# A decoder layer on one core: the first attention's feature maps shared between VectorE and GpSimd

## What is computed

```python
def _feature_map(t, K):                       # 16 heads of 64
    f = jnp.einsum('hdf,bhld->bhlf', K, t)
    feats = jnp.concatenate([jax.nn.softmax(f, axis=-1), jax.nn.softmax(-f, axis=-1)], axis=-1)
    return jnp.maximum(feats, EPS)
q, k, v = _heads(x @ Wq), _heads(x @ Wk), _heads(x @ Wv)
qf, kf = _feature_map(q, Kq), _feature_map(k, Kk)
kv = jnp.cumsum(kf[:, :, :, None, :] * v[..., None], axis=2)
o = jnp.einsum('bhlf,bhldf->bhld', qf, kv)
z = jnp.einsum('bhlf,bhlf->bhl', qf, jnp.cumsum(kf, axis=2)) + EPS
y = heads_joined(o / z[..., None]) @ Wo       # x = x + y
```

## Time and profile before

| | |
|---|---|
| median of 3 runs | 1230.46 us (1229.52 to 1231.06) |
| the profiled execution | 1229.25 us, span 1227.0 us |
| the first attention | about 540 us of it |
| TensorE clock granted, mean | 0.982 of full speed |
| busy share of the span | TensorE 91%, VectorE 78%, ScalarE 50%, GpSimd 31% |

### The profile page before, as it was taken

How to read it: one execution, slowest core, us unless ns; L and a number is a source line. 1 busy time by engine, 2 the same in 40 slices (tenths; PEclk the granted TensorE clock), 3 DMA queues, 4 the chain that set the end, 5 groups by cost and what they waited for, 6 DMA issues and landing times. The chain is left out here.

```text
span 1227.0 us, 30062 instructions
## 1 busy us (share of the span) xinstructions
PE 1117.3 (91%) x11860; PEld 719.6 (59%) x11861; DVE 962.1 (78%) x1769; ACT 611.1 (50%) x1166; POOL 377.3 (31%) x355
## 2 busy tenths in 40 slices
PE   6698898899899999879999999999999957999996
PEld 5577777777788878643443344334444334666765
DVE  6889978987888788888788677877889556777757
ACT  4233343334333433227777677776788822444443
POOL 4432245222522222113201320222110414656651
PEclk9899999999999999999999999999999988999998
DMA  7100001000400000524720570065050144221225
GB/s 240 41 8 1 2 28 53 2 1 1 80 2 2 1 1 2 81 59 81 152 34 8 114 146 2 9 127 108 2 211 3 53 80 145 65 64 60 63 62 205
DMA packets 60045, 73.65 MB, mean 60 GB/s; under 512 B 14404, under 2 KB 51140, under 8 KB 59188
## 3 DMA queue, kind: packets, MB, share of 16 engines
q1 hardware_dynamic: 56132, 61.56, 21.0%
q0 software_dynamic: 3792, 10.36, 2.7%
HBM read 52.86 MB, written 18.78 MB: 58 GB/s over the span
## 5 line engine op out<-in xcount | busy, mean ns | idle before, releaser
L1791 DVE TENSOR_REDUCE neg_max<-pS 128x1 f32<-128x1024 f32 x238 | 284.9, 1220 | 56.2 <-PE pS L1574 56.0
L1706 ACT ACTIVATE pt<-pR 128x512 f32<-128x512 f32 x512 | 286.5, 600 | 80.1 <-PE pR L1597 75.3
L1597 PE MATMUL pR<-qs,ks 100*32 100x512 bf16 x2048 | 191.2, 383 | 3.1 <-ACT pt L1706 1.6
L1574 PE MATMUL pS<-ks,qs 100*32 100x512 bf16 x1904 | 145.9, 381 | 5.1 <-issue 1.9
L1611 PE MATMUL b_pO<-pt,b_v 128*32 128x512 f32 x1024 | 135.9, 605 | 2.9 <-ACT pt L1706 2.3
L1597 PEld LDWEIGHTS pR<-qs,ks 100*32 100x32 bf16 x2048 | 56.2, 96 | 95.3 <-issue 25.6
L324 POOL TENSOR_TENSOR kf<-kf,fsum 128x2048 f32<-128x2048 f32 (+1 forms) x17 | 58.2, 3422 | 163.8 <-DVE fsum L933 163.8
L324 POOL TENSOR_TENSOR qs<-qs,fsum 128x2048 f32<-128x2048 f32 (+1 forms) x17 | 58.5, 3446 | 142.7 <-DVE fsum L933 142.7
L1453 POOL COPY qs<-max_rows 3x512 bf16<-3x512 bf16 x60 | 36.6, 610 | 209.3 <-ACT max_rows L1699 206.3
L745 ACT COPY qfT<-pT 128x512 f32<-128x512 f32 x64 | 37.3, 582 | 122.7 <-PE pT L466 122.7
L1574 PEld LDWEIGHTS pS<-ks,qs 100*32 100x32 bf16 x1904 | 51.4, 97 | 74.3 <-issue 35.7
(11 more groups left out here) (376 smaller groups left out, 2270.8 us busy)
## 6 DMA issues: line engine op xcount, KB each, us to landing
qs<-q_scr SPq DMA_DIRECT2D x24, 256.0 KB
ks<-k_scr SPq DMA_DIRECT2D x7, 768.0 KB
k_scr<-f SPq DMA_DIRECT2D x18, 256.0 KB, 2.8
ks<-in_L_ffn_w_dram SPq DMA_DIRECT2D x2, 2048.0 KB, 11.1
ks<-in_L_ffn_w_dram SPq DMA_DIRECT2D x4, 1024.0 KB, 8.5
ks<-y_rows SPq DMA_DIRECT2D x16, 256.0 KB, 5.1
ks<-k_scr SPq DMA_DIRECT2D x6, 512.0 KB
cx<-in_ctx_dram SPq DMA_DIRECT2D x3, 768.0 KB, 12.3
```

What stands on the lines that cost most here:

```text
L1574: ins = pe.matmul(pS1[q:q + XV, slot, 512 * half:512 * half + 512], qs[0:KR, bass.ds(par, 1), h, P * t + q:P * t + q + XV].rearrange("r a ...
L1597: ins = pe.matmul(ring[bank][q:q + XV, :], ks[0:KR, bass.ds(par, 1), h, P * j + q:P * j + q + XV].rearrange("r a n -> r (a n)"), qs[0:KR, ...
L1706: nc.scalar.activation(pt[:, j % 2, i, :], ring[bank], ACT.Exp).then_inc(exp_done, 1)
L1791: nc.vector.tensor_reduce(neg_max[:, hg % 2, u // G, u % G:u % G + 1], pS1[:, u % 2, :], AX_X, ALU.max, negate=True).then_inc(max_done, 1)
```

## The change

From tile 2 of the keys and tile 1 of the queries on, VectorE writes only the positive side, and min - max of each head; GpSimd makes the negative side as (min - max) - (f - max) from it, in SBUF (`other_side`), and ScalarE's exponentials wait for that. A new semaphore `drained` frees the half of `pP` for TensorE as soon as VectorE has read it. GpSimd also takes the clamps of all tiles but 0; the queries' product and clamp are done in halves of eight heads. VectorE's clamps leave its loop. The keys' sums stood ahead of the residual and the mask in the kernel before as well (L1121).

```diff
+        low_less_high = sb("low_less_high", [P, 2, H])
+        drained = [sem("k_drained"), sem("q_drained")]
+        POOL_FROM = (2, 1)
+        def bank_drained(eng, m, t, half_of):
+            if t < POOL_FROM[m]:
+                eng.wait_ge(shifted[m], 2 * t + half_of + 1)
+            else:
+                eng.wait_ge(drained[m], 2 * (t - POOL_FROM[m]) + half_of + 1)
...
+                def scaled_after(m, t, part):
+                    if m == 1:
+                        return 2 * t + part + 1
+                    return t + part + 1 if t == 0 else t + 2
+                def clamp(m, t, par, hs=slice(0, H), part=1):
+                    pool.wait_ge(scaled[m], scaled_after(m, t, part))
+                    nc.gpsimd.tensor_scalar(feat[m][:, par, hs], feat[m][:, par, hs], FEAT_EPS, None,
+                                            ALU.max).then_inc(f_ready[m], 1)
+                def other_side(m, t, half_of, par):
+                    pool.wait_ge(drained[m], 2 * (t - POOL_FROM[m]) + half_of + 1)
+                    hs = slice(8 * half_of, 8 * half_of + 8)
+                    nc.gpsimd.tensor_tensor(feat[m][:, par, hs, HD:F2],
+                                            low_less_high[:, m, hs].unsqueeze(2).broadcast_to([P, H // 2, HD]),
+                                            feat[m][:, par, hs, 0:HD], ALU.subtract).then_inc(shifted[m], 1)
...
-                        if not (last and c == TB - 1):
-                            scale(1, TB * b + c + 1, (c + 1) % 2)
+                        if has1:
+                            other_side(1, t + 1, 0, 1 - par)
+                            clamp(0, t + 1, 1 - par)
+                            other_side(1, t + 1, 1, 1 - par)
+                            for half_of, hs in enumerate(HALVES):
+                                scale(1, t + 1, 1 - par, hs, half_of)
+                                clamp(1, t + 1, 1 - par, hs, half_of)
                         if (b, c) == (0, TB - 1):
                             split_k(0)
                             split_k(1)
-                        if not (last and c >= TB - 2):
-                            scale(0, TB * b + c + 2, c % 2)
+                        if has2:
+                            other_side(0, t + 2, 0, par)
+                            other_side(0, t + 2, 1, par)
+                            scale(0, t + 2, par)
...
                 def project_q(t, half, par):
-                    wait(pe, shifted[0], 2 * t + half + 1)
+                    bank_drained(pe, 0, t, half)
...
-                    nc.vector.tensor_tensor(feat[m][:, par, hs, 0:HD], f,
-                                            hi[:, m, hs].unsqueeze(2).broadcast_to([P, H // 2, HD]), ALU.subtract)
+                    if t >= POOL_FROM[m]:
+                        nc.vector.tensor_tensor(low_less_high[:, m, hs], lo[:, m, hs], hi[:, m, hs], ALU.subtract)
+                    ins = nc.vector.tensor_tensor(feat[m][:, par, hs, 0:HD], f,
+                                                  hi[:, m, hs].unsqueeze(2).broadcast_to([P, H // 2, HD]),
+                                                  ALU.subtract)
+                    if t >= POOL_FROM[m]:
+                        ins.then_inc(drained[m], 1)
+                        return
...
-                            if g == 1 and has1:
-                                clamp(0, t + 1, 1 - par)
...
-                            if g == G - 1 and has1:
-                                clamp(1, t + 1, 1 - par)
```

More of the change, by code:

```diff
@@ L320, in scale @@
                 def scale(m, t, par, hs=slice(0, H), part=1):
-                    wait(pool, summed[m], t + part + 1)
+                    wait(pool, summed[m], t + part + 1 if t == 0 else t + 2)
                     e = feat[m][:, par, hs].rearrange("p h (s f) -> p (h s) f", s=2)
@@ L377, in batch @@
                                                     ).then_inc(x1_norm, 1)
-                        if not (last and c == TB - 1):
-                            scale(1, TB * b + c + 1, (c + 1) % 2)
+                        t, par = TB * b + c, c % 2
+                        has1, has2 = not (last and c == TB - 1), not (last and c >= TB - 2)
+                        if has1:
[5 more added lines that the diff above has]
+                                clamp(1, t + 1, 1 - par, hs, half_of)
                         if (b, c) == (0, TB - 1):
@@ L448, in project_q @@
                 def project_q(t, half, par):
-                    wait(pe, shifted[0], 2 * t + half + 1)
+                    bank_drained(pe, 0, t, half)
                     project(1, half, par, proj[1])
                 def project_v(t, half, par):
-                    wait(pe, shifted[1], 2 * t + half + 1)
+                    bank_drained(pe, 1, t, half)
                     project(2, half, par, v_proj)
@@ L458, in transposes @@
                     for m in (1, 0):
-                        if t == 0 and g % 2 == 0:
-                            wait(pe, f_ready[m], g // 2 + 1)
+                        if m == 1 and g % 2 == 0:
+                            pe.wait_ge(f_ready[m], 2 * t + g // 2 + 1)
+                        elif t == 0 and g % 2 == 0:
+                            pe.wait_ge(f_ready[m], g // 2 + 1)
                         elif g == 0:
-                            wait(pe, f_ready[m], t + 2)
+                            pe.wait_ge(f_ready[m], t + 2)
+                        if g == 0:
                             wait(pe, oT_ready, 2 * t)
@@ L927, in denominators @@
                     if t:
-                        wait(dve, scaled[m], t + 1)
+                        wait(dve, scaled[m], 2 * t if m == 1 else t + 1)
                     d = fsum[:, m, 2 * hs.start:2 * hs.stop]
```

## The result

The changed kernel takes 1318.65 us (median of 4 runs, 1315.38 to 1319.62), the kernel before 1229.99 beside it (4 runs, 1229.06 to 1231.06). The ratio is 1.0716, with a 95% interval of 1.0695 to 1.0737: 7.2% slower, or 88.7 us by the medians. The forecast was 1246.8 with a range up to 1258. The sign was right and the size wrong by a factor of five. The profiled execution has a span of 1316.1 us, against 1227.0 before.

What follows compares the result with a forecast made beforehand. The prediction took TensorE, nearly full at 91% busy, as the bound, with VectorE binding tiles 1 and 2. Its tile terms summed to +16.3 us on 1229.25, giving 1245.6; with 1.2 for the median, 1246.8, range 1235 to 1258.

Steps and rivals of the forecast that it cites:

- predicted +6.4: Tiles 4 and 8: negative query side issued behind two splits on GpSimd, clamp of 2.3 us included; +6.4 us each.
- price of a side: GpSimd's negative side of 512 columns, from the line through two product prices: 1.04 us.
- balance of the ordinary tiles: Later mask +0.35 us against state wait gone -0.55: -0.2 in tiles 6 and 10, 0 in 7 and 11.
- The rival in which the relief wins: Queue effects cost little and state waits of 12.4 us go: -10 us, 1220; chance 0.10.
- GpSimd's prices: GpSimd's clamp, priced between memset and two-input rows: 2.3 us whole, 1.45 a half.
- Behind the sums: After the query sums, half products and clamps take 6.8 us on GpSimd; first key side needed some 7 later: just hidden.
- two-input price adds about 9.5: Range term: clamps at the two-input price add about 9.5 us, 1.3 in tiles 0, 4, 5, 8, 9, 13.
- relief of tiles 1 and 2: Tiles bound by VectorE, making mask rows too; shorter state and mask waits give -2.7 and -2.0 us.
- the last pair: Last two tiles: waits for the first row maximum (1.17) and the state (0.4) shrink, about 1.5 us gained.
- Contention: VectorE and GpSimd block each other; by it alone tiles 5, 9 and 13 would each cost some 0.3 us more.

Runs made afterwards that it cites:

- The first experiment: Changed kernel with both clamps back on VectorE and the query product whole again, GpSimd keeping the negative sides: 1247.10 us, ratio 1.0108.
- the splits' order: Kernel with only the negative sides on GpSimd, the splits of tiles 4 and 8 moved behind the query sides: 1240.21 us, ratio 1.0073.
- two-input price: Changed kernel with GpSimd's clamp replaced by a two-tensor addition of the clamp's constant over the same columns: 1281.51 us, ratio 1.0389.
- normalisation later: Changed kernel with VectorE's normalisation issued one head group later, behind the division of group 1: 1304.99 us, ratio 1.0567.
- the clamps only: Changed kernel with the negative sides back on VectorE, GpSimd keeping the clamps: 1234.74 us, ratio 1.0014.
- sides, query clamp: Changed kernel with the keys' clamp back on VectorE, GpSimd keeping the negative sides and the queries' clamp: 1263.24 us, ratio 1.0269.
- clamp behind sides: Changed kernel with GpSimd's keys' clamp placed behind both negative query sides instead of between them: 1273.98 us, ratio 1.0342.
- key clamp, norm. later: Kernel with negative sides and only the keys' clamp on GpSimd, VectorE's normalisation moved behind the division of group 1: 1300.13 us, ratio 1.0559.
- sides, key clamp: Changed kernel with the queries' clamp back on VectorE, GpSimd keeping the negative sides and the keys' clamp: 1306.52 us, ratio 1.0621.
- those of the key sums: VectorE's key sums moved behind residual, mask and statistics: on the kernel before 1230.17 us; on the sides-only kernel with splits behind the sides 1251.18 us.

## Why the prediction was wrong in size

**What held.** The order of the mechanism: a negative side behind other work in GpSimd's queue delays the exponential, then the sums, the mask and TensorE. The first experiment gives 1247 for the sides, and the splits' order alone gives back 5 us in tile 4 and 4.6 in tile 8. That their +6.4 and +6.0 equal the predicted +6.4 is luck, since no clamp stands in them. The price of a side (1.04) held, and so did the balance of the ordinary tiles as long as the clamps stay on VectorE: tiles 6 and 7 changed by -0.2 and +0.1 (unrounded) with the sides alone, where -0.2 and 0 were predicted. The rival in which the relief wins is excluded by the time. The relief is not nothing: with the sides alone TensorE's waits for the state fell from 12.4 us (7.5 and 4.9 in the earlier trace rows) to 6.0. In the changed kernel they are 15.7 and 6.8.

The stage by groups of tiles, each against the kernel before, in us (the two last columns are taken from the residual additions; tile 0 is what is lost ahead of the first of them):

```
tiles             predicted   two-input price   changed
0                   +2.4          +6.6           +9.6
1, 2                -4.7          +1.5           +7.1
3                   +4.1          +7.0          +10.5
4, 8               +12.8         +16.6          +22.8
5, 9, 13            +4.4         +13.0          +20.1
6, 7, 10, 11        -0.4          +6.1          +13.5
12                  -0.7          +3.2           +6.0
14, 15              -1.5          -0.1           +3.1
sum                +16.3         +53.9          +92.6
```

**"GpSimd's prices" failed.** The clamp is 5.36 us, not 2.3, and a half 2.77, not 1.45. The upper end was wrong too: the product with two inputs was taken to bound an instruction with one. By the addition in the clamp's place, the part above the two-input price is worth about 40 us; by the table of stretches below, 23 of the 36 us that it adds to the stage are TensorE's busy time, that is the clock's.

**"Behind the sums" failed with it.** Products and clamps in halves last 9.5 us against 6.8, and the key sides come behind them: the query clamp adds 1.6% over the sides.

**The range's "two-input price adds about 9.5" failed on its own.** With the step at 3.61 us the loss is 48, where the sum gave 26. By the table, tiles 4 and 8 are then nearly right (8.3 each, where 7.7 were predicted at that price), and what is missing lies elsewhere. First, in the ordinary tiles the clamp between the two query sides was left out, as if the second side did not want GpSimd until the clamp had ended: tiles 6, 10 and 12 lose 2.8, 2.8 and 3.2 us (7 and 11, which have no state update, 0.4 and 0.1). At the prediction's own 2.3 us this would have cost next to nothing (an estimate: with the normalisation later, a clamp of 2.3 from 288.43 would end at 290.73, and the side's values, but for the hold, would be there at about 290.7); so the omission and the wrong price hang together. Second, the relief of tiles 1 and 2, put at -4.7, and of the last pair, at -1.5, did not come. The two state waits of the earlier trace rows stand at 1.71 and 1.56 us with the sides alone, as they stood before, and no kernel gained more than 0.7 us in tiles 1 and 2 together, or 1.3 in the last pair. Why they stayed was not looked for.

**The clamp's place was worth as much as its price.** Moving the clamp behind the second query side, at its full price, takes back 3.8% (7.2 to 3.4), 46 us, some 4 in eleven of the tiles (tile 6 goes from 34.8 to 31.1). The lower price in the old place took back 40. The two overlap and don't add up: what is lost is a wait as long as the clamp, at the one place where the query side needs the queue. Which part of that is GpSimd's queue and which is VectorE held beside the clamp is parted only roughly: moving the normalisation gave 14 to 18 of the 46 us and left other holds in place.

**"Contention" failed by its size and by its place.** It was priced at 0.3 us in tiles 5, 9 and 13 and left out of the sum. The normalisation was held 5.2 us beyond its 0.40 in tiles 1, 2, 6, 10 and 12, and a row of the keys' mask took 5.73 us beside a clamp in tile 3 (2.60 at most before); the prediction had expected less of this, since VectorE's clamps leave. By the runs that put the normalisation later, its place is worth 14 to 18 us in the changed kernel and 6 to 8 with the keys' clamp alone. With the clamps only, the whole change costs 0.1% (0.5 at most), holds of 2.78 to 7.42 us with it. So it seems that the holding counts where VectorE then makes what GpSimd's queue and TensorE wait for; no run parts it further.

**The clock was not priced.** The stretch from the first residual to the last, split as above into TensorE's idle and busy time:

```
                          us      idle    busy    granted clock
before                    455.1    40.7   414.4   1.00
sides only                471.3    50.6   420.7   0.97
sides, query clamp        484.5    62.4   422.1   0.98
clamp behind sides        494.4    69.3   425.1   0.96
two-input price           502.4    79.1   423.3   0.97
key clamp, norm. later    515.6    76.8   438.8   0.93
normalisation later       523.8    82.6   441.1   0.93
sides, key clamp          528.1    84.9   443.2   0.92
changed                   538.0    91.3   446.7   0.92
```

Idle time grows, and busy time jumps: by 15.5 us between the fifth row and the sixth, though the sixth has 2.3 us less of idle time. The last four rows are the kernels in which the clamp of 5.36 us stands between the query sides. TensorE's single waits of 3 us or more number 0, 2, 3, 5 and 4 in the first five rows, and 7, 8, 12 and 14 in the last four. So the number of long waits, rather than the sum of all, goes with the lower clock. Smaller differences of busy time mean little here: the kernels without any such wait, those of the key sums among them, lay between 414 and 425 us. Moving the clamp behind the sides gave back 22.0 us of idle and 21.6 us of busy time.

Together, by the ratios: sides 13 us, clamps 2, and 73 from having both on GpSimd at once: the queue, the holding and the clock's part within them. The orders tried take back up to 46 of those 73. Products and clamps that cross from one tile into the next still hold the key sides; a kernel with all orders changed at once was not tried. None of the kernels beat the one before by more than 0.2%.

## What to carry to other kernels

A busy share of 31% says that an engine has room, not that it has it when a step on the path comes: before moving a step that others wait for, write down what stands ahead of it in that engine's queue in every tile, and count its longest instruction as a possible wait. Price an operation from a row of its own kind, not from one that seems harder, and where there is no such row, measure one first. When two parts of a change are cheap alone, still run them together: here 0.1% and 1.1% made 7.2%.

## What the runs showed of the hardware

**GpSimd's one-input maximum is dearer than its two-input product** (float32, in place; the product's second input is one column for each 64): 5.36 us and 3.62 for 128x2048, 2.77 and 1.90 for 128x1024.

**GpSimd holds some VectorE instructions, as a rule until its own ends.** The normalisation (L939; ns, min/median/max) in the changed kernel:

```profile
L939 DVE TENSOR_SCALAR a_xn<-xr,a_mv,a_rstd x16: 402/748/5600, 12.2 to 543.2; 128x256 f32<-128x256 f32 x16
```

Its longest value is not a slower pace: it ends 0.15 us behind the clamp. The maxima that read PSUM and the sums were not held (0.67 us beside GpSimd's work as without it, and 2.29 for the sum that starts at 284.23 in the run with the clamp behind the sides, within the clamp's 282.36 to 287.72). The Trainium skill (SBUF — State Buffer, SBUF: two separate sides) says that the pair of ports that both engines share is an exclusive lock for a whole instruction, taken by whoever starts first, for VectorE's two-port modes and for its instructions with two SBUF inputs. The trace agrees for the normalisation, 5.60 for 0.40, and for the difference beside a product, 1.95 for 0.17; but the normalisation has the earlier start in the profile, 296.43 against 296.52, so who comes first can't be read from the starts alone. And beside a clamp the difference is let go earlier, as in tile 7 of the changed kernel:

```profile
331.31 5.40 POOL L345 TENSOR_SCALAR kf<-kf 128x2048 f32<-128x2048 f32 x1
```

```profile
332.78 2.22 DVE L961 TENSOR_TENSOR low_less_high<-lo,hi 128x8 f32<-128x8 f32 x1
```

It ends at 335.00, 3.69 us behind the clamp's start, and the clamp runs on to 336.71. In the four cases of this kernel that is 3.65 to 3.71 us behind the start, so here "the whole instruction" does not fit. No run shows why.

**TensorE's clock was lower behind long gaps.** The same eight score matmuls of the changed kernel, in tile 6 behind a short gap, and in tile 4 behind 4.70 us of waiting. The rows of the stretches above give their granted clocks, 1.00 and 0.66:

```profile
291.57 1.13 PE L516 MATMUL pA<-qfT,kfT 128*128 128x128 f32 x8 [0.72 <-DVE am L990]
...
227.80 2.07 PE L516 MATMUL pA<-qfT,kfT 128*128 128x128 f32 x8 [4.70 <-ACT kfT L786]
```

1.13 us is the level of 2.4 GHz and 2.07 that of 1.2. Behind the gap of 3.25 us in tile 6 the stretch from 304 to 310 us was granted 0.72; there the eight score matmuls directly behind the gap still took 1.13 us (at 304.76), and only those after them were slow. A wait on the path is therefore paid twice here: once as idle time, 50.6 us in the stage, and once in the work behind it, 32.3 us.
